# A shared ring of three bank pairs and wide exponentials in two attention stages, with the two kinds of score units in turn

## The reference

```
def _L1_attn_ref(x, w_qkv, w_proj, b_proj):
    qkv = (x @ w_qkv.T).reshape(B, N, 3, HEADS, HEAD_DIM)
    q, k, v = (qkv[:, :, 0], qkv[:, :, 1], qkv[:, :, 2])
    attn = jnp.einsum('bnhd,bmhd->bhnm', q * scale, k)
    attn = jax.nn.softmax(attn, axis=-1)
    out = jnp.einsum('bhnm,bmhd->bnhd', attn, v).reshape(B, N, C)
    return out @ w_proj.T + b_proj

def _L3_attn_ref(x, w_qkv, w_proj):          # q, k, v as above
    attn = jnp.where(causal, jnp.einsum('bhqd,bhkd->bhqk', q, k) * scale, -jnp.inf)
    a = jnp.clip(attn, -100.0, 100.0)
    e = jnp.exp(a - jnp.max(a, axis=-1, keepdims=True))
    p = e / (jnp.sum(e, axis=-1, keepdims=True) + 1e-06) + 1e-08
    attn = p / jnp.sum(p, axis=-1, keepdims=True)
    ...
```

## Time and profile before

| | us |
|---|---|
| median of 3 runs | 2062.26 (2058.0 to 2062.41) |
| the profiled execution's own time | 2065.93 |
| its span, from the first to the last instruction | 2063.8 |
| busy in the span: PE, DVE, ACT, POOL | 1671.3, 1394.2, 1009.2, 414.3 |
| first to last addition L724, self stage | 311.3 to 534.4 |
| first to last addition L724, causal stage | 1487.7 to 1763.8 |

### The profile page before, as it was taken

One profiled execution on the slowest core, in us unless ns is written; L12 is line 12 of the kernel. 1 busy time (PEld: TensorE's weight loads), 2 busy tenths in 40 slices (PEclk: granted clock), 3 DMA queues, 4 the chain that ended last, 5 costly groups with the idle time before them and its releaser, 6 DMA issues. The chain is left out here.

```text
span 2063.8 us, 32418 instructions
## 1 busy us (share of the span) xinstructions
PE 1671.3 (81%) x11422; PEld 990.5 (48%) x11422; DVE 1394.2 (68%) x3239; ACT 1009.2 (49%) x2161; POOL 414.3 (20%) x575
## 2 busy tenths in 40 slices
PE   5779859999878999957789999973587878798692
PEld 3546533333365666645544444531344444365582
DVE  4646678888584777765566767767788889665434
ACT  3336536666523554535355555542245545465362
POOL 1110030000034666541200000001200000100375
PEclk9989869999989999987799999995688999999797
DMA  4100021221046888850000000000211110000213
GB/s 116 41 1 2 1 71 61 63 62 31 1 165 256 333 326 328 324 180 1 1 1 1 1 1 1 1 1 18 71 56 58 32 58 16 1 2 14 94 53 84
DMA packets 71545, 151.09 MB, mean 73 GB/s; under 512 B 9042, under 2 KB 55419, under 8 KB 66299
## 3 DMA queue, kind: packets, MB, share of 16 engines
q1 hardware_dynamic: 61211, 136.25, 19.0%
q0 software_dynamic: 4992, 10.23, 1.6%
q10 hardware_dynamic: 5184, 2.55, 0.5%
HBM read 124.46 MB, written 29.26 MB: 74 GB/s over the span
## 5 line engine op out<-in xcount | busy, mean ns | idle before, releaser
L162 POOL TENSOR_SCALAR rstd<-MV 128x2 f32<-128x2 f32 (+1 forms) x100 | 25.9, 259 | 999.7 <-DVE MV L130 995.0
L640 ACT ACTIVATE l1aE<-PS 128x512 f32<-128x512 f32 x256 | 142.2, 596 | 75.5 <-PE PS L543 72.9
L701 DVE TENSOR_REDUCE l1aM<-PS 128x2 f32<-128x1024 f32 x128 | 150.4, 1218 | 26.2 <-PE PS L515 24.6
L640 ACT ACTIVATE l3aE<-PS 128x512 f32<-128x512 f32 (+3 forms) x256 | 102.7, 439 | 111.7 <-PE PS L545 108.8
L2582 ACT COPY PT<-PS 128x512 f32<-128x512 f32 x128 | 69.2, 589 | 93.5 <-PE PS L2493 93.2
L701 DVE TENSOR_REDUCE l3aM<-PS 128x2 f32<-128x256 f32 (+3 forms) x128 | 100.2, 817 | 15.7 <-PE PS L517 15.5
L2672 DVE TENSOR_REDUCE M<-PS 128x1 f32<-128x589 f32 x128 | 92.5, 764 | 27.0 <-PE PS L2482 26.7
L1713 PE MATMUL PS<-WB,H 128*128 128x512 f32 x234 | 107.4, 595 | 0.0
L2588 ACT ACTIVATE E<-PS,M 128x589 f32<-128x589 f32 x128 | 95.9, 763 | 17.6 <-DVE M L2672 17.5
L543 PE MATMUL PS<-l1aQS,l1aKS 128*128 128x512 bf16 x256 | 90.6, 388 | 8.5 <-ACT l1aE L640 7.0
L729 DVE SCALAR_TENSOR_TENSOR l3aE<-l3aE,l3aLB 128x2048 f32<-128x2048 f32 (+1 forms) x64 | 94.9, 1482 | 2.7 <-ACT l3aE L640 2.7
(11 more groups left out here) (671 smaller groups left out, 4273.1 us busy)
## 6 DMA issues: line engine op xcount, KB each, us to landing
WB<-in_experts SPq DMA_DIRECT2D x39, 1286.0 KB
TB<-mixed_tails SPq DMA_DIRECT2D x39, 768.5 KB, 7.1
l1aQS<-head_image SPq DMA_DIRECT2D x16, 256.0 KB, 2.9
l1aKS<-head_image SPq DMA_DIRECT2D x32, 128.0 KB, 3.0
l3aQS<-head_image SPq DMA_DIRECT2D x16, 256.0 KB, 2.9
l3aKS<-head_image SPq DMA_DIRECT2D x32, 128.0 KB, 3.1
head_image<-l1aparts SPq DMA_DIRECT2D x8, 384.0 KB, 2.5
head_image<-l3aparts SPq DMA_DIRECT2D x8, 384.0 KB, 2.5
```

What stands on the lines that cost most here:

```text
L640: nc.scalar.activation(E[:, place(m, kt) + j, q0:S], PS[:, 4 + n % 2, q0:S], ACT.Exp, scale=SCALE).then_inc(exp_done, 1)
L701: v.tensor_reduce(M[:, m % 2, qt, 2 * hp:2 * hp + 2], PS[:, bank:bank + 2, 0:kc], AX, ALU.max, negate=True).then_inc(pair_free, 1)
```

## The change

Six things change in `attention16`, and nothing in the other stages:

1. `A`, `T`, `B` and `L` share one ring of three bank pairs (banks 0 to 5): each takes the next pair, once the unit three places back has been read.
2. `B` and `L` come for two heads at a time, and ACT does one exponential of up to 1024 columns where it did two of up to 512. A group has 8 `B`.
3. In the self stage `KS` has no zero halves: the two heads of a pair are 64 rows each, and a pair's two matmuls use the upper and the lower half of the array's rows. One DMA loads it where two did.
4. The tables are plain: `B` of one group and `A` of the next in turn, `V` whole at one place, `P` and `T` at the end.
5. `P` goes from DVE to POOL, as do the last step of the split of the projections from the second batch on, and the sums of values in the causal stage.
6. `E` holds five key tiles instead of three; clearing of `Va` on DVE stands behind the first projections' split; the clearing of `KS` on POOL falls away in the self stage.

The diff, cut to its core (the tables in full):

```diff
 CAUSAL = (
-    ('L', 0, 0, 0), ('L', 0, 0, 1), ('V', -1, 2, 1), ('A', 1, 0, 0), ('X', -1, 3), ('L', 0, 0, 2), ('A', 1, 1, 0), ('L', 0, 0, 3),
...
-    ('B', 0, 3, 2), ('V', 0, 1, 1), ('A', 2, 0, 1), ('B', 0, 3, 3), ('A', 2, 1, 1),
+    ('L', 0, 0), ('L', 0, 1), ('V', -1, 0, 4), ('B', 0, 0, 0), ('A', 1, 0, 0), ('B', 0, 0, 1), ('A', 1, 0, 1), ('F', -1), ('X', 0, 0),
+    ('B', 0, 1, 0), ('A', 1, 1, 0), ('B', 0, 1, 1), ('A', 1, 1, 1), ('X', 0, 1), ('B', 0, 2, 0), ('A', 1, 2, 0), ('B', 0, 2, 1),
+    ('A', 1, 2, 1), ('X', 0, 2), ('B', 0, 3, 0), ('A', 1, 3, 0), ('B', 0, 3, 1), ('A', 1, 3, 1), ('X', 0, 3), ('P', 1), ('T', 1),
 )
 FULL = (
-    ('B', 0, 0, 0), ('B', 0, 0, 1), ('V', -1, 2, 2), ('B', 0, 0, 2), ('A', 1, 0, 0), ('B', 0, 0, 3), ('B', 0, 1, 0), ('A', 1, 1, 1),
...
-    ('B', 0, 3, 2), ('A', 2, 1, 0), ('B', 0, 3, 3), ('A', 2, 2, 0),
+    ('V', -1, 0, 4), ('B', 0, 0, 0), ('A', 1, 0, 0), ('B', 0, 0, 1), ('A', 1, 0, 1), ('F', -1), ('B', 0, 1, 0), ('A', 1, 1, 0),
+    ('B', 0, 1, 1), ('A', 1, 1, 1), ('B', 0, 2, 0), ('A', 1, 2, 0), ('B', 0, 2, 1), ('A', 1, 2, 1), ('B', 0, 3, 0), ('A', 1, 3, 0),
+    ('B', 0, 3, 1), ('A', 1, 3, 1), ('P', 1), ('T', 1),
 )
...
+    SLOTS, SETS = 3, 5
+    rows_of = lambda par: slice(0, P) if causal else slice(64 * par, 64 * par + 64)
...
+    pairs = [u for u in order if u[0] in "ABLT"]
+    slot_of = {u: i % SLOTS for i, u in enumerate(pairs)}
+    slot_prev = {u: pairs[i - SLOTS] for i, u in enumerate(pairs) if i >= SLOTS}
...
-                if u in ut:
-                    n = ut[u]
-                    bank = 2 * (n % 2)
-                    if n >= 2:
-                        emptied(pairs[n - 2])
+                if u in slot_of:
+                    bank = 2 * slot_of[u]
+                    if u in slot_prev:
+                        emptied(slot_prev[u])
...
-                    if kt == 0 and j == 0:
-                        pe.wait_ge(pair_free, ut[("T", m)] + 1)
+                    if u == first_b[m]:
+                        pe.wait_ge(pair_free, ut["T", m] + 1)
...
+                elif kind == "P":
+                    pool.wait_ge(pair_free, ut[last_a[m]] + 1)
+                    ...
+                    step(g.tensor_copy(high, maxima))
+                    step.wait()
+                    step(g.tensor_tensor(rest, maxima, high, ALU.subtract))
+                    step.wait()
+                    step(g.tensor_copy(middle, rest))
+                    step.wait()
+                    g.tensor_tensor(low, rest, middle, ALU.subtract).then_inc(max_split, 1)
...
-                        nc.scalar.activation(E[:, place(m, kt) + j, q0:S], PS[:, 4 + n % 2, q0:S], ACT.Exp, scale=SCALE).then_inc(exp_done, 1)
+                        q0, at = kt * P if causal else 0, place(m, kt) + 2 * hp
+                        nc.scalar.activation(E[:, at:at + 2, q0:S], PS[:, bank:bank + 2, q0:S], ACT.Exp, scale=SCALE).then_inc(exp_done, 1)
```

More of the change, by code:

```diff
@@ L390, in attention16 @@
     ut, ub = (count([u for u in order if u[0] in kinds]) for kinds in ("AT", "BL"))
+    pairs = [u for u in order if u[0] in "ABLT"]
+    slot_of = {u: i % SLOTS for i, u in enumerate(pairs)}
+    slot_prev = {u: pairs[i - SLOTS] for i, u in enumerate(pairs) if i >= SLOTS}
     uj = count([u for u in order if u[0] == "J" and u[2] not in (2, 4)])
-    pairs = list(ut)
+    first = lambda kinds: {m: next(u for u in pairs if u[0] in kinds and u[1] == m) for m in range(NG)}
+    first_a, first_b = first("A"), first("BL")
     last_a = {u[1]: u for u in ut if u[0] == "A"}
+    last_b = {u[1]: i for u, i in ub.items() if u[0] == "B"}
+    last_exp = {u[1:3]: i + 1 for u, i in ub.items() if u[0] == "B"}
+    last_low = {u[1]: i + 1 for u, i in ub.items() if u[0] == "L"}
     singles = [u for u in order if u in uj or u[0] in "FCWN"]
-    ring = (7, 4, 5, 6)
+    ring = (7, 6, 5, 4)
     bank_of, bank_prev, users = {}, {}, {}
@@ L451, in _ @@
                 sp.dma_start(QS[:, own, :], k.image[b, 0, heads].rearrange("(a r) d j s -> (r d j) a s", r=2)).then_inc(stacked[g], 16)
-                for par in range(2):
-                    sp.dma_start(KS[64 * par:64 * par + 64, own, par, :], key[par]).then_inc(stacked[g], 16)
+                if causal:
+                    for par in range(2):
+                        sp.dma_start(KS[64 * par:64 * par + 64, own, par, :], key[par]).then_inc(stacked[g], 16)
+                else:
+                    sp.dma_start(KS[:, own, :], k.image[b, 1, heads].rearrange("(a r) d j s -> (r d j) a s", r=2)).then_inc(stacked[g], 16)
         @block.tensor
@@ L514, in _ @@
                         o = PS[:, bank + par, 0:kc]
-                        ins = mm(o, QS[:, pp, qt * P:(qt + 1) * P], KS[:, pp, par, 0:kc], start=True, stop=not causal)
+                        own = rows_of(par)
+                        key = KS[:, pp, par, :] if causal else KS[own, pp, :]
+                        ins = mm(o, QS[own, pp, qt * P:(qt + 1) * P], key[:, 0:kc], start=True, stop=not causal)
                         if causal:
@@ L525, in _ @@
                 elif kind in "BL":
[L526 to L533, removed]
-                    if kt == 0 and j == 0:
-                        pe.wait_ge(pair_free, ut[("T", m)] + 1)
[L536 to L545, removed]
+                    hp = u[-1]
+                    if u == first_b[m]:
+                        pe.wait_ge(pair_free, ut["T", m] + 1)
+                    pp = 2 * g + hp
+                    for par in range(2):
+                        o = PS[:, bank + par, :]
+                        if kind == "L":
+                            ins = mm(o, k.maxrows[:, par, :], QS[:, pp, :], start=True, stop=True)
+                        else:
+                            kt = u[2]
+                            q0 = kt * P if causal else 0
+                            own = rows_of(par)
+                            key = KS[:, pp, par, :] if causal else KS[own, pp, :]
+                            ins = mm(o[:, q0:S], key[:, kt * P:(kt + 1) * P], QS[own, pp, q0:S], start=True, stop=not causal)
+                            if causal:
+                                ins = mm(o[:, q0:q0 + P], k.ident_b, k.causalT_b, start=False, stop=True)
                     ins.then_inc(s_ready, 1)
@@ L550, in _ @@
                     for kt in range(u[2], u[2] + u[3]):
+                        if m == 0 and kt == 0 and 6 in users:
+                            emptied(users[6])
                         if kt == 0 and g == 0:
@@ L602, in _ @@
             g = nc.gpsimd
[L603 to L606, removed]
             g.memset(Mp[:, :, :, :], 0.0).then_inc(zeroed, 1)
-            for b in range(BT):
-                k.norm_gpsimd(pool, b, b)
+            if causal:
+                pool.wait_ge(zeroed, 1)
+                g.memset(KS[P // 2:P, :, 0, :], 0.0).then_inc(zeroed, 1)
+                pool.wait_ge(zeroed, 2)
+                g.memset(KS[0:P // 2, :, 1, :], 0.0).then_inc(zeroed, 1)
@@ L732, in _ @@
                     dve.wait_ge(o_turned, m + 1)
+                    if causal and g == 0:
+                        dve.wait_ge(v_summed, b + 1)
                     turned_o = PS[:, bank_of[u], :].rearrange("p (t j d) -> p t j d", t=NT, j=HG)
```

132 lines of the change are left out of this document (71 added, 61 removed), and 5 rows, old and new, of tables (CAUSAL, FULL).

## The result

2257.1 us (median of 4 runs, 2249.2 to 2260.1), against 2061.5 for the kernel before beside it: ratio 1.0943, 95% interval 1.0922 to 1.0965. The profiled execution took 2260.1 us, span 2258.2. The two windows from the first to the last addition, and the additions (L750 now), answer to the earlier trace rows.

A forecast was written before the change was run, and what follows sets the result against it. DVE was taken as fed nearly without a break, by the old order. The profiled 2065.9 us, +94 (self) and +136 (causal) gave 2296, less 3.7 for the median: 2292 us; range 2205 to 2350 at 0.85.

The forecast's parts named there:

- Order and turn: Both attention stages: reductions, then split, T, V and first scores one after another, leaving DVE a hole of about 9 us.
- 15 x 19.65 and 15 x 25.8: Self and causal windows: 16 additions taken as 15 equal periods of 19.65 and 25.8 us, batch work on top.
- The self period of 19.65: Self stage, one group: reductions and split to 13.05 us, T 0.9, V 5.7; 17.3 to 21.55 by clock.
- The split on POOL: Between last reduction and T: four POOL operations, 1.75 us plus 0.2 hand-over; 1.2 to 2.0 us named as sign.
- The clock: PE while waiting for the split: T and first part of V at 1.2 GHz, mean granted clock 0.6 to 0.85.
- the rival with the clock up: PE in both windows: clock does not fall, 2062 + 58 + 94 = 2214 us; chance 0.15.
- The causal period of 25.8: Causal stage, one group: loop 15.0, split to 17.3, addition to 19.5, two L to 21.3, V 4.5 us.
- Batch work: Projections, output and norm, on top of the periods: 22 us in the self stage, 25 in the causal.
- Wide exponentials and row halves: Self loop: a wide exponential takes 1.03 us; a pair of half-row matmuls costs one pass, 0.22 us (0.43 at 1.2 GHz).
- PE was not the limit: Rival, self stage: PE is the real limit, freeing 3.5 us a group outweighs the turn, 2006 us; chance 0.05.
- drain at a change of tiling: Rival, PE: each tiling change empties the array, 0.2 us; 2285 to 2308 us, counted within the likeliest case's 0.62.
- the ends: Starts and ends of both stages: 1 us saved at each start, the last group's drain takes as much, 0.

The follow-up runs named there:

- the good order on the new ones: Changed kernel with three A units run two groups ahead, V in pieces, and the causal stage's batch work behind T: 2033.6 us, ratio 0.9882.
- split_dve: Changed kernel with the split (P) moved back from POOL to DVE at the same place in the order: 2234.0 us, ratio 1.0843.
- old_parts_plain_order: Kernel before with its old parts, given only the change's plain order and 5 sets of exponentials in place of 3: 2264.8 us, ratio 1.0993.
- the filled run: Changed kernel with matmuls that nothing reads, issued before the waits of T and the first L: 2187.1 us, ratio 1.0607.
- the four lookahead runs: Changed kernel in four orders running A units two groups ahead, placing V, F and batch work differently: 2105.5, 2055.9, 2062.9 and 2033.6 us.
- lookahead2: Changed kernel, A units two groups ahead, V in smaller pieces, last causal A and P ahead of the first clip, W behind P and T: 2055.9 us.
- lookahead3: lookahead2 with the batch work moved and spread over four groups, and F ahead of the first clip in causal attention: 2062.9 us, ratio 0.9997.

## Why the prediction came out as it did

The mechanism was right and the time was in the range; the sum was 35 us too high. By its own steps:

- **Order and turn.** Right: PE, in its order, puts split, `T` and `V` in a row, and DVE idles there, 8.8 us around one addition where about 9 were named. The plain order on the old parts (2264.8) and the good order on the new ones (2033.6) show that it is the order. That holds for the total. By stage the new parts cost 14 us in self attention and save 11 in causal attention in the plain order, which the prediction didn't tell apart.
- **15 x 19.65 and 15 x 25.8.** The mis-sized factor. The first period of a stage has no `V` of a group before: it took 14.65 us and 20.19 us. That makes the sum 5.0 + 5.6 us too high.
- **The self period of 19.65.** The five periods without any batch work average 18.53 us (starts of the additions). In the group shown the loop took 10.6 us (470.68 to 481.30) where 11.1 was forecast: the second reduction starts 0.2 us sooner than was laid out, `F` adds 0.4 instead of 0.6, and the forecast's own terms add up to 11.0. The way from the last reduction to `T` took 1.5 (1.95 forecast), `T` 0.9 as forecast, `V` 5.73 (5.7). Over the window `V` averages 75.2/(452/32) = 5.3. The forecast is 14 x 1.12 = 16 us too high.
- **The split on POOL.** Sized too high: 0.24 to 0.27 us an operation where I took 0.45 for the two-tensor ones from wide shapes (the rows' slope gives 0.48, and 0.28 stood for the 0.24 of a one-tensor one; the two slips cancel). The four add up to 1.02 us, under the 1.2 to 2.0 named as a sign. The Trainium skill, GPSIMD Engine Reference, section 4.1, advises VectorE for elementwise work, and its direction held: split_dve is 17.5 us faster in the two windows. Its factor of two for two inputs did not hold on 16 columns: 0.24 and 0.27 us here against 0.19 (old_parts_plain_order) and 0.23 on DVE.
- **The clock.** Right, and dear: `T` (1.01 us where the filled run has 0.62) and a part of `V` run at 1.2 GHz. In the group shown the granted clock is 0.50 from 463 to 469, while `T` and most of `V` run, and 1.00 from 469.3 to 472. The mean granted clocks of the windows, 0.81 and 0.78, lie in the forecast range. Filling the wait took 70 us off, close to the 78 between the forecast and the rival with the clock up.
- **The causal period of 25.8.** The five periods without any batch work average 24.95 us. In them the loop took 14.4 on average (15.0 forecast) and `V` 4.1 (4.5). In the turn shown it is 2.26 from the start of the last clip to `T` (2.3 forecast), 2.5 from `T` to `L` (2.2), and 1.8 for two `L` (1.75). The forecast is 14 x 0.85 = 12 us too high in all.
- **Batch work.** What is left of the windows is 21.4 us (22 forecast) and 29.9 (25): in the causal stage the forecast is 5 us too low.
- **Wide exponentials and row halves.** 1.03 us and one pass, as taken; undone, neither moves the kernel's time by more than the intervals.
- **The rivals.** PE was not the limit: in the self window it is busy 199.8 us instead of 206.0, and the window grew by 72.4. No drain at a change of tiling is seen between `V` and `B`: by the profile, which models the ends of matmuls, `B` starts where `V` ends, and the first reduction, whose start is not modelled, follows 0.58 us later (0.65 forecast without a drain). For the other changes of tiling no such price is shown either way.

Together -21 and -13 us against +94 and +136; the ends are -1.3 instead of 0.

## What to carry to other kernels

In a kernel whose engines run in order, write the list of each engine for one period and look for the stretch in which one engine's last result is the next one's first input: everything else has to be placed beside that stretch before any instruction is made shorter. An idle PE cost twice here, by the wait and by the clock of the matmuls behind it. A total that stays the same can hide stages that moved in opposite directions, so compare by stage. A period that is multiplied by its count should be checked at its ends: the first and last rounds often lack a term.

## What the runs showed of the hardware

An operation of POOL on 16 columns that starts while a clip runs on DVE (two operands in SBUF) ends only behind the clip. In the traces of the changed kernel and the four lookahead runs there are 80 such operations of the causal split, and all 80 end 0.10 to 0.14 us behind the clip beside them. With the clamp L680, the first operation of that split, beside the clip (lookahead2, POOL and DVE):

```profile
1725.79 2.17 POOL L680 TENSOR_SCALAR l3aM<-l3aM 128x16 f32<-128x16 f32 x1 [13.56 <-DVE l3aM L782]
...
1729.02 0.30 POOL L690 TENSOR_TENSOR l3aMp<-l3aMleft,l3aMp 128x16 bf16<-128x16 f32 x1
```
```profile
1725.56 2.28 DVE L794 SCALAR_TENSOR_TENSOR l3aE<-l3aE,l3aLB 128x2048 f32<-128x2048 f32 x1
```

With `F` moved ahead of the clips (lookahead3) the clamp takes 0.26 us, and the last operation of the split, now beside the first of two clips, 2.13:

```profile
1521.13 0.26 POOL L680 TENSOR_SCALAR l3aM<-l3aM 128x16 f32<-128x16 f32 x1 [14.67 <-DVE l3aM L782]
...
1522.48 2.13 POOL L690 TENSOR_TENSOR l3aMp<-l3aMleft,l3aMp 128x16 bf16<-128x16 f32 x1
```
```profile
1522.20 3.99 DVE L794 SCALAR_TENSOR_TENSOR l3aE<-l3aE,l3aLB 128x2048 f32<-128x2048 f32 x2
```

The Trainium skill, SBUF — State Buffer, section "Who interferes with whom", says that a VectorE instruction with two SBUF inputs contends with a GpSimd instruction that reads SBUF. These rows agree, by 2.17 against 0.26 us, and the prediction had left it out; in the changed kernel it cost little (the clamp at 0.64), because only the last, short clip ran beside the split.
